# Expert routing of a two-layer block: three bits per round, tile sums by matmul, one-hots of 128 places

## The chip, the cores and the metric

The kernel runs on one core of one Trainium2 chip. A core has a matrix engine (TensorE, PE in the rows, with its weight loads as PEld), VectorE (DVE), ScalarE (ACT), GpSimd (POOL) and SyncE (SP), which here only issues transfers; they share the on-chip SBUF, and TensorE's results stand in PSUM. Engines run their own instruction streams and wait for each other by semaphores. The metric is the device time of the whole kernel in microseconds (us), the median of several executions.

## The reference, cut to what matters

Two layers, each of an attention part and a mixture of eight experts in which every expert picks its tokens. Only the picking is touched by the change:

```python
# layer 0: k = N / E = 256 (softmax over experts, then top_k over tokens); layer 1: k = 2 N / E = 512
route_prob = jax.nn.softmax(xf @ Ws + bs, axis=-1).T      # [E = 8, N = 2048]
route_vals, routes = jax.lax.top_k(route_prob, k)         # per expert: k values and token numbers
xin = xf[routes]
h = jax.nn.gelu(jnp.einsum('ekd,edf->ekf', xin, W1) + b1[:, None, :])
out = jnp.einsum('ekf,efd->ekd', h, W2) + b2[:, None, :]
final = jnp.zeros((N, D)).at[routes.reshape(-1)].add((out * route_vals[..., None]).reshape(-1, D))
```

The order of the tokens within an expert's list doesn't matter, since each result is added back at its token's row. On a tie the lower token number comes first.

## The kernel before

`program` calls one phase after the other: projections, attention, `out_stage` (which leaves the router's logits in `logits`, 128 partitions x 16 tiles of tokens x 8 experts), `route`, `experts`, and the same again for the second layer. Each phase is a block with one hand-written instruction stream per engine, and ends with a barrier of all engines. There is no scheduler: instructions run on each engine in the order in which they are written, and `link(op)` makes VectorE wait for its own operation before the next one starts.

`route` (lines 1069 to 1239) is called with k = 256 (`route0`) and k = 512 (`route1`). Its stream on VectorE:

- softmax over the experts, with the exponential on ScalarE (L1156 to L1162), and the constants `digits` (L1168), 15 multiplications of 128x32.
- Bisection for each expert's k-th largest probability (L1171 to L1183). Probabilities are compared as float32 whose bit pattern is built from the top: two bits in a round, 15 rounds. A round makes four candidates per expert (`cand`), compares all probabilities with them (`above`, 128 x 4 x 16 x 8), lets TensorE sum over partitions and tiles by 16 matmuls with a matrix of ones into `tot` (L1128), keeps the candidates that at least k tokens reach (`passed`) and takes the largest (`kth`).
- Masks of the larger (`ge`) and equal (`eq`) probabilities; `need` is how many of the equal ones are taken.
- `ranks` (L1194 to L1206), called twice: TensorE gives the rank within a tile (`pre`, with a triangular matrix) and each tile's sum (`col`); VectorE adds the sums of earlier tiles by a scan in four doubling steps. The result `pos` is each chosen token's place in its expert's list, -1 for the others.
- The records `rec` (L1219 to L1225), five bfloat16 values for each token and expert: the number within the tile, the tile, the probability in three parts.
- The lists (L1226 to L1239): for each of 8 experts and 16 tiles a one-hot matrix `hot` of 128 tokens x k places (L1230) compares the constant row `slot` (0, 1, 2, ... in float16) with `pos`; TensorE multiplies it, 128 places at a time, with the records (L1142) and sums over the tiles. `hot` has two buffers, and VectorE fills the next expert's while TensorE reads. From `lists` VectorE makes `index` and `weight`, which `experts` reads.

## Time and profile before

| | us |
|---|---|
| median of three timed runs | 4181.79 (4180.73 to 4182.9) |
| the profiled execution | 4189.89 |
| its span, first to last instruction | 4188.3 |
| mean granted TensorE clock | 0.935 of full speed |
| first routing, from its first VectorE operation to its last | 1753.7 to 1828.5 |
| second routing | 3323.6 to 3408.0 |

Times are microseconds from the start of the span. A row of the timeline gives an operation's start, its duration and, in brackets, how long its engine had stood idle before it and who ended that. Operations of one kind in a row are merged (x16), and then the time is that of the whole group. Durations of operations that follow each other without waiting overlap, so the distance between two of them is read from their starts or ends. `128x512 bf16<-128x512 f32` is the shape and type of output and input.

### The profile page before, as it was taken

To read this page: it belongs to the slowest core of one execution; us is meant where nothing else is said; L and a number is where in the kernel's file an instruction comes from. 1 tells how busy PE (TensorE), PEld (TensorE's weight loads), DVE (VectorE), ACT (ScalarE), POOL (GpSimd) and SP (SyncE) were. 2 spreads that over 40 slices of the span, in tenths; PEclk is the share of its full clock that TensorE was granted. 3 is DMA by queue.
4 is the path that set the end of the run, shared out by engine and by line. 5 is a ranking of instruction groups with operands and counts; after the bars stand their busy time and mean duration, and the time that the engine had idled before them with its cause. 6 is when DMAs were issued, how large, how long until landed. Compare 5 with 4: busy or idle time off the path is not lost. (4 is left out here: it accounts for less than half of the span.)

```text
span 4188.3 us, 77504 instructions
## 1 busy us (share of the span) xinstructions
PE 3748.4 (89%) x30860; PEld 2629.4 (63%) x30860; DVE 2555.5 (61%) x3210; ACT 2014.6 (48%) x3511; POOL 1739.5 (42%) x854
## 2 busy tenths in 40 slices
PE   7989799999999996649996699999997649999997
PEld 5768456666666563448995355555553438888886
DVE  4345778888888772566664677777772564433342
ACT  2222266666666662036662366666663024444442
POOL 0000287778777872001110488888884001111110
PEclk9999799999999998669998799999999659999999
DMA  4478624442444223236663522232202233333341
GB/s 161 169 247 284 182 61 106 103 112 63 105 103 112 58 65 117 101 134 205 210 188 111 146 77 77 78 81 78 77 22 80 98 105 120 115 113 113 113 117 29
DMA packets 287917, 485.16 MB, mean 116 GB/s; under 512 B 22289, under 2 KB 117521, under 8 KB 285585
## 3 DMA queue, kind: packets, MB, share of 16 engines
q1 hardware_dynamic: 272016, 443.00, 35.5%
q0 software_dynamic: 14080, 37.76, 3.9%
q8 instruction: 205, 3.36, 0.4%
q14 instruction: 80, 0.65, 0.1%
q10 hardware_dynamic: 1536, 0.40, 0.0%
HBM read 350.67 MB, written 130.02 MB: 115 GB/s over the span
## 5 line engine op out<-in xcount | busy, mean ns | idle before, releaser
L844 DVE TENSOR_REDUCE attn_parts<-attn_mx 128x4 f32<-128x2048 f32 x538 | 1232.6, 2291 | 378.3 <-PE attn_mx L686 378.0
L803 ACT ACTIVATE attn_probs<-attn_low 128x512 f32<-128x512 f32 (+1 forms) x2368 | 1235.1, 595 | 473.0 <-PE attn_low L714 353.2
L665 POOL TENSOR_TENSOR attn_psums<-attn_psums,attn_probs 128x1024 f32<-128x1024 f32 x536 | 1275.2, 2379 | 70.0 <-ACT attn_probs L803 4.8
L714 PE MATMUL attn_low<-attn_queries,attn_keys 97*128 97x256 f32 (+1 forms) x4736 | 917.7, 312 | 13.6 <-ACT attn_probs L803 5.2
L714 PEld LDWEIGHTS attn_low<-attn_queries,attn_keys 97*128 97x128 f32 x4736 | 660.7, 190 | 373.3 <-ACT attn_probs L803 188.8
L731 PE MATMUL attn_low<-attn_probs,attn_values 128*32 128x256 f32 x9472 | 632.2, 385 | 1.4 <-ACT attn_probs L803 1.4
L1462 DVE TENSOR_TENSOR ffn_wL<-ffn_raw,ffn_wH 128x2048 fp32r<-128x2048 f32 x128 | 293.4, 2292 | 224.2 <-ACT ffn_wH L1417 222.9
L1417 ACT ACTIVATE ffn_wH<-ffn_raw 128x2048 fp32r<-128x2048 f32 x128 | 245.2, 1916 | 339.1 <-DMA ffn_raw<-in_L_ffn_W_dram 178.3
L662 POOL TENSOR_TENSOR attn_psums<-attn_probs 128x1024 f32<-128x1024 f32 x88 | 209.6, 2382 | 380.0 <-ACT attn_probs L803 380.0
L731 PEld LDWEIGHTS attn_low<-attn_probs,attn_values 128*32 128x32 f32 x9472 | 248.2, 109 | 183.8 <-issue 3.9
L1374 PE MATMUL ffn_up<-ffn_xH,ffn_wH 128*128 128x256 f32 (+1 forms) x1024 | 350.6, 342 | 2.7 <-DVE ffn_xL L1468 2.7
L686 PE MATMUL attn_mx<-attn_keysn,attn_queriesn 32*128 32x512 f32 (+3 forms) x2388 | 299.6, 494 | 53.1 <-DMA attn_queriesn<-l_queries 28.3
L1374 PE MATMUL ffn_up<-ffn_xH,ffn_wL 128*128 128x256 f32 (+1 forms) x1024 | 346.7, 339 | 0.0
L1374 PE MATMUL ffn_up<-ffn_xL,ffn_wH 128*128 128x256 f32 (+1 forms) x1024 | 346.7, 339 | 0.0
L1389 PE MATMUL ffn_down<-ffn_wH,ffn_hH 128*128 128x512 f32 x768 | 306.7, 399 | 0.0
L1389 PE MATMUL ffn_down<-ffn_wH,ffn_hL 128*128 128x512 f32 x768 | 304.4, 396 | 0.0
L1389 PE MATMUL ffn_down<-ffn_wL,ffn_hH 128*128 128x512 f32 x768 | 304.3, 396 | 0.0
L1343 POOL DMA_INDIRECT out_dram<-ffn_yo,ffn_idx_out x32 | 52.6, 1643 | 594.6 <-DVE ffn_yo L1497 463.5
L738 PE MATMUL attn_low<-attn_probs,keep_onesf 128*32 128x256 f32 (+1 forms) x3776 | 268.5, 375 | 0.0
L1486 DVE TENSOR_TENSOR ffn_hL<-ffn_hf,ffn_hH 128x256 fp32r<-128x256 f32 (+1 forms) x256 | 138.1, 555 | 202.5 <-ACT ffn_hH L1438 199.8
L861 DVE RECIPROCAL attn_inv<-attn_both 128x64 f32<-128x64 f32 x384 | 200.7, 535 | 70.8 <-ACT attn_both L812 70.8
L1438 ACT ACTIVATE ffn_hf<-ffn_up,ffn_b1T 128x256 f32<-128x256 f32 (+1 forms) x256 | 149.2, 583 | 160.7 <-PE ffn_up L1374 156.7
(196 smaller groups left out, 4457.2 us busy)
## 6 DMA issues: line engine op xcount, KB each, us to landing
ffn_raw<-in_L_ffn_W_dram SPq DMA_DIRECT2D x128, 1024.0 KB, 5.6
attn_keys<-l_cross_keys SPq DMA_DIRECT2D x96, 512.0 KB, 6.8
attn_queries<-l_queries SPq DMA_DIRECT2D x48, 512.0 KB, 4.8
l_cross_keys<-projc_high SPq DMA_DIRECT2D x64, 256.0 KB
l_cross_keys<-projc_lowp SPq DMA_DIRECT2D x64, 256.0 KB
l_cross_values<-projc_vout SPq DMA_DIRECT2D x64, 256.0 KB
attn_keysn<-l_cross_keys SPq DMA_DIRECT2D x16, 1024.0 KB, 5.1
attn_values<-l_cross_values SPq DMA_DIRECT2D x32, 512.0 KB, 6.7
```

The costliest lines, as they stand in the source:

```text
L662: pool.tensor_tensor(ps, probs[:, m % RING, 0, :, :], at, ALU.add).then_inc(added, 1)
L665: pool.tensor_tensor(ps, ps, at, ALU.add).then_inc(added, 1)
L686: mm = pe.matmul(room[:, h, at:at + cols], QN[b][rows_h, q0:q0 + P], KN[b][rows_h, part * BLK:part * BLK + cols], start=True, stop=True)
L714: mm = pe.matmul(out[:, n0:], KS[b][0:3 * HD + 1, h, kb * P:(kb + 1) * P], QS[b][0:3 * HD + 1, h, job.qb * QB + n0:(job.qb + 1) * QB], sta ...
L731: mm = pe.matmul(acc[h * HD:(h + 1) * HD, 0, n0:], VS[b][:, kb, h * HD:(h + 1) * HD], probs[:, m % RING, i, h, n0:], start=kb == 0, stop=k ...
L738: mm = pe.matmul(acc[h * HD:(h + 1) * HD, 1, n0:], c["onesf"][:, 0:HD], probs[:, m % RING, i, h, n0:], start=False, stop=False, skip_group ...
L803: act.activation(probs[:, m % RING, i // 2, heads, n0:], sc[:, item % SC, :].rearrange("p (h q) -> p h q", q=QB)[:, :, n0:], ACT.Exp, scal ...
L844: op = dve.tensor_reduce(into, seen, AX.X, ALU.max)
L1374: mm = pe.matmul(up[ft % UP][:, 0:k], w[:, cols], x[:, ch, :], start=n == 0, stop=n == 3 * C - 1)
L1389: mm = pe.matmul(down[st][:, :], h[:, ft, st * P:(st + 1) * P], w[:, cols], start=ft == 0 and n == 0, stop=ft == FT - 1 and n == 2)
L1417: act.activation(wH[:, m % RING, :], raw[:, m % RING, :], ACT.Copy).then_inc(high_made, 1)
L1462: dve.tensor_tensor(wL[:, m % RING, :], raw[:, m % RING, :], wH[:, m % RING, :].bitcast(F32), ALU.subtract).then_inc(low_made, 1)
```

## The change

Only `route` is changed. The bisection takes three bits in a round (`WAYS` = 8 candidates, 10 rounds). `digits` is computed by GpSimd. The masks are written directly as bfloat16. The sums of earlier tiles are added by TensorE: after the triangular matmul, 15 matmuls with ones add each tile's mask to all later tiles in `pre`; `col` and the scan are gone. A token's place is split into `part` (which 128 places of the list) and `place` (0 to 127 in it). The one-hots have 128 places for either k. The records are copied ST = k/128 times, each copy multiplied by whether the token belongs to that part (`recs`), and one matmul for expert and tile gives all parts side by side. `hot` has room for all experts. Experts 6 and 7 are made by ScalarE from `less` = -`place`: |slot - place| by Abs, then max(0, 1 - that) by Relu, each pair with a wait in between. Part of the records' work moves to before the waits for TensorE.

```diff
-    ROUNDS = 15
+    BITS, ROUNDS = 3, 10
+    WAYS = 1 << BITS
+    BY_ACT = (6, 7)
...
+        recs = ph.sb("recs", [P, NTILE, E, ST, NV], BF16)
         tok = ph.sb("tok", [P, 2, NTILE], I32)
-        hot = ph.sb("hot", [P, 2, NTILE, k], BF16)
+        hot = ph.sb("hot", [P, E, NTILE, P], BF16)
+        gap = ph.sb("gap", [P, 2, P])
...
             @block.gpsimd
             def _(pool):
-                pool.iota(digit[:, :, :], pattern=[[1, 4], [0, E]], base=0, channel_multiplier=0)
+                pool.iota(digit[:, :, :], pattern=[[1, WAYS], [0, E]], base=0, channel_multiplier=0).then_inc(numbered, 1)
+                pool.wait_ge(numbered, 1)
+                for n in range(ROUNDS):
+                    pool.tensor_scalar(digits[:, n, :, :], digit[:, :, :], float(WAYS ** (ROUNDS - 1 - n)), None, ALU.mult
+                                       ).then_inc(digits_set, 1)
...
                 act.activation(prob[:, :, :], rest[:, :, :], ACT.Exp).then_inc(expd, 1)
+                act.wait_ge(placed, 1)
+                n = 0
+                for e in BY_ACT:
+                    for t in range(NTILE):
+                        act.activation(gap[:, n % 2, :], c["slot"][:, 0:P], ACT.Abs, bias=less[:, t, e:e + 1]
+                                       ).then_inc(gap_set, 1)
+                        act.wait_ge(gap_set, n + 1)
+                        act.activation(hot[:, e, t, :], gap[:, n % 2, :], ACT.Relu, scale=-1.0, bias=c["onesf"][:, 0:1]
+                                       ).then_inc(hot_act, 1)
+                        n += 1
...
-                for n in range(2):
-                    pe.wait_ge(counted, ROUNDS + 2 + n)
-                    pe.matmul(pre[:, :, :], c["lowerb"][:, :], maskb[:, :, :], start=True, stop=True)
-                    pe.matmul(col[:, :, :], c["onesb"][:, :], maskb[:, :, :], start=True, stop=True
-                              ).then_inc(summed, 1)
+                for n, mask in ((2, eqb), (3, selb)):
+                    pe.wait_ge(counted, ROUNDS + n)
+                    pe.matmul(pre[:, :, :], c["lowerb"][:, :], mask[:, :, :], start=True, stop=False, skip_group_check=True)
+                    for t in range(NTILE - 1):
+                        mm = pe.matmul(pre[:, t + 1:, :], c["onesb"][:, :],
+                                       mask[:, t, :].unsqueeze(1).to_broadcast([P, NTILE - 1 - t, E]),
+                                       start=False, stop=t == NTILE - 2, skip_group_check=True)
+                    mm.then_inc(summed, 1)
+                pe.wait_ge(recs_set, ST)
                 for e in range(E):
-                    pe.wait_ge(hot_ready, e + 1)
-                    for st in range(ST):
-                        for t in range(NTILE):
-                            mm = pe.matmul(lists[:, e, st, :], hot[:, e % 2, t, st * P:(st + 1) * P],
-                                           rec[:, t, e, :], start=t == 0, stop=t == NTILE - 1)
-                    mm.then_inc(hot_used, 1)
+                    if e in BY_ACT:
+                        pe.wait_ge(hot_act, NTILE * (BY_ACT.index(e) + 1))
+                    else:
+                        pe.wait_ge(hot_ready, e + 1)
+                    for t in range(NTILE):
+                        mm = pe.matmul(lists[:, e, :, :], hot[:, e, t, :], recs[:, t, e, :, :],
+                                       start=t == 0, stop=t == NTILE - 1)
+                mm.then_inc(hot_used, 1)
...
+                dve.wait_ge(summed, ROUNDS + 2)
+                link(dve.tensor_tensor(pos[:, :, :], pre[:, :, :], over_tokens(need[:, :]), ALU.is_lt))
+                link(dve.tensor_tensor(pos[:, :, :], pos[:, :, :], eqb[:, :, :], ALU.mult))
+                dve.tensor_tensor(selb[:, :, :], pos[:, :, :], geb[:, :, :], ALU.add).then_inc(counted, 1)
...
+                dve.wait_ge(summed, ROUNDS + 3)
+                link(dve.scalar_tensor_tensor(out=pos[:, :, :], in0=pre[:, :, :], scalar=1.0, in1=selb[:, :, :],
+                                              op0=ALU.add, op1=ALU.mult))
+                link(dve.tensor_scalar(part[:, :, :], pos[:, :, :], float(P + 1), None, ALU.is_ge))
+                for st in range(2, ST):
+                    link(dve.scalar_tensor_tensor(out=part[:, :, :], in0=pos[:, :, :], scalar=float(st * P + 1),
+                                                  in1=part[:, :, :], op0=ALU.is_ge, op1=ALU.add))
+                link(dve.scalar_tensor_tensor(out=rest[:, :, :], in0=part[:, :, :], scalar=float(-P), in1=pos[:, :, :],
+                                              op0=ALU.mult, op1=ALU.add))
+                link(dve.tensor_scalar(less[:, :, :], rest[:, :, :], -1.0, 1.0, ALU.mult, ALU.add))
+                dve.tensor_scalar(place[:, :, :], rest[:, :, :], -1.0, None, ALU.add).then_inc(placed, 1)
+                for st in range(ST):
+                    dve.scalar_tensor_tensor(out=recs[:, :, :, st, :],
+                                             in0=part[:, :, :].unsqueeze(3).to_broadcast([P, NTILE, E, NV]),
+                                             scalar=float(st), in1=rec[:, :, :, :], op0=ALU.is_equal, op1=ALU.mult
+                                             ).then_inc(recs_set, 1)
+                dve.wait_ge(placed, 1)
                 for e in range(E):
-                    if e >= 2:
-                        dve.wait_ge(hot_used, e - 1)
+                    if e in BY_ACT:
+                        continue
                     for t in range(NTILE):
-                        op = dve.tensor_scalar(hot[:, e % 2, t, :], c["slot"][:, 0:k], pos[:, t, e:e + 1], None,
+                        op = dve.tensor_scalar(hot[:, e, t, :], c["slot"][:, 0:P], place[:, t, e:e + 1], None,
                                                ALU.is_equal)
                     op.then_inc(hot_ready, 1)
```

How the engines' streams read at two places of the first routing (names are of tiles, `route_` for this phase, `keep_` for what outlives it). VectorE before, from the end of the second `ranks` to the copy of the lists:

```order
L1206 TENSOR_TENSOR route_pos<-route_scan,route_pre 128x128
L1215 TENSOR_SCALAR route_pos<-route_pos 128x128
L1216 TENSOR_TENSOR route_pos<-route_pos,route_sel 128x128
L1217 TENSOR_SCALAR route_pos<-route_pos 128x128
L1219 CAST route_rec<-route_tok 128x128
L1220 CAST route_rec<-route_tok 128x128
L1221 CAST route_rec<-route_prob 128x128
L1222 TENSOR_TENSOR route_rest<-route_prob,route_rec 128x128
L1223 CAST route_rec<-route_rest 128x128
L1224 TENSOR_TENSOR route_rest<-route_rest,route_rec 128x128
L1225 CAST route_rec<-route_rest 128x128
L1230 TENSOR_SCALAR route_hot<-keep_slot,route_pos 128x256 x128
```

VectorE now, from the last part of the records (which stands behind the mask of the chosen tokens) to the copy of the lists:

```order
L1221 CAST route_rec<-route_rest 128x128
L1225 SCALAR_TENSOR_TENSOR route_pos<-route_pre,route_selb 128x128
L1227 TENSOR_SCALAR route_part<-route_pos 128x128
L1231 SCALAR_TENSOR_TENSOR route_rest<-route_part,route_pos 128x128
L1233 TENSOR_SCALAR route_less<-route_rest 128x128
L1234 TENSOR_SCALAR route_place<-route_rest 128x128
L1236 SCALAR_TENSOR_TENSOR route_recs<-route_part,route_rec 128x128x5 x2
L1245 TENSOR_SCALAR route_hot<-keep_slot,route_place 128x128 x96
L1249 COPY route_got<-route_lists 128x80
```

The records now come ahead of the places, two masked copies of them stand behind, and 96 one-hots of 128 places take the place of 128 of 256 (in the second routing, of 512, with four copies).

ScalarE before, from the exponential into the experts phase:

```order
L1121 ACT_TABLE_LOAD
L1121 ACTIVATE route_prob<-route_rest 128x128
L1111 UNCONDITIONAL_BRANCH
L1402 UNCONDITIONAL_BRANCH
L1417 ACTIVATE ffn_wH<-ffn_raw 128x2048 x3
```

ScalarE now at the same place, up to the first of 32 pairs:

```order
L1124 UNCONDITIONAL_BRANCH
L1127 ACT_TABLE_LOAD
L1127 ACTIVATE route_prob<-route_rest 128x128
L1132 ACTIVATE route_gap<-keep_slot,route_less 128x128
L1135 ACTIVATE route_hot<-route_gap,keep_onesf 128x128
```

The pairs stand behind the exponential in the same phase; the number of table loads is the same as before.

## Rows read from the trace of the kernel before

**Rows 1.** page: span; then busy us (share) xinstructions of each engine
```profile
span 4188.3 us, 77504 instructions
...
PE 3748.4 (89%) x30860; PEld 2629.4 (63%) x30860; DVE 2555.5 (61%) x3210; ACT 2014.6 (48%) x3511; POOL 1739.5 (42%) x854
```

**Rows 2.** stretches: start:end length, busy (xinstructions), clock, DMA share, GB/s
```profile
1753.60:1828.60 75.00, 18.25 (x501) 15.39 (x501) 58.05 (x256) 1.59 (x2) 0.36 (x3) 0.50 0.00 1
3323.60:3408.10 84.50, 25.07 (x757) 22.21 (x757) 66.78 (x256) 1.57 (x2) 0.35 (x3) 0.50 0.01 1
...
3371.00:3406.40 35.40, 14.94 (x512) 14.27 (x512) 33.48 (x128) 0.00 (x0) 0.00 (x0) 0.50 0.01 2
```

**Rows 3.** timeline, one round: start, us, engine line op out<-in xcount [idle]
```profile
1759.72 0.19 DVE L1173 TENSOR_TENSOR route_cand<-route_digits,route_kth 128x32 int32<-128x32 int32 x1
1759.94 0.69 DVE L1175 TENSOR_TENSOR route_above<-route_prob,route_cand 128x512 bf16<-128x512 f32 x1
...
1760.69 0.61 PE L1128 MATMUL route_tot<-route_above,keep_onesb 128*128 128x32 bf16 x16 [1.48 <-DVE route_above L1175]
1761.34 0.19 DVE L1181 SCALAR_TENSOR_TENSOR route_passed<-route_tot,route_cand 128x32 f32<-128x32 f32 x1 [0.71 <-PE route_tot L1128]
```

**Rows 4.** timeline, VectorE, constants and first candidates
```profile
1756.21 1.37 DVE L1168 TENSOR_SCALAR route_digits<-route_digit 128x32 int32<-128x32 int32 x15
1757.53 0.07 DVE L1170 MEMSET route_kth<- 128x8 int32 x1
1757.62 0.19 DVE L1173 TENSOR_TENSOR route_cand<-route_digits,route_kth 128x32 int32<-128x32 int32 x1
```

**Rows 5.** timeline, VectorE, last threshold to one-hots, first routing
```profile
1788.96 0.29 DVE L1186 TENSOR_TENSOR route_ge<-route_prob,route_kth 128x128 f32<-128x128 f32 x1
...
1789.61 0.38 DVE L1189 TENSOR_REDUCE route_count<-route_ge 128x8 bf16<-128x128 f32 x1
...
1798.70 0.34 DVE L1219 CAST route_rec<-route_tok 128x128 bf16<-128x128 int32 x1
1798.84 0.38 DVE L1220 CAST route_rec<-route_tok 128x128 bf16<-128x128 int32 x1
...
1800.86 25.16 DVE L1230 TENSOR_SCALAR route_hot<-keep_slot,route_pos 128x256 bf16<-128x256 f16 x128
```

**Rows 6.** timeline, lists' end of routing one; one-hots, end of two
```profile
1826.07 1.01 PE L1142 MATMUL route_lists<-route_rec,route_hot 128*128 128x5 bf16 x32 [2.12 <-DVE route_hot L1230]
1827.13 0.24 DVE L1234 COPY route_got<-route_lists 128x80 f32<-128x80 f32 x1 [1.11 <-PE route_lists L1142]
...
3370.79 33.69 DVE L1230 TENSOR_SCALAR route_hot<-keep_slot,route_pos 128x512 bf16<-128x512 f16 x128
...
3404.54 1.87 PE L1142 MATMUL route_lists<-route_rec,route_hot 128*128 128x5 bf16 x64 [2.33 <-DVE route_hot L1230]
3406.44 0.33 DVE L1234 COPY route_got<-route_lists 128x160 f32<-128x160 f32 x1 [1.96 <-PE route_lists L1142]
```

**Rows 7.** groups by line and shape, VectorE: xcount | busy us, mean ns
```profile
L1462 DVE TENSOR_TENSOR ffn_wL<-ffn_raw,ffn_wH 128x2048 fp32r<-128x2048 f32 x1 | 2.3, 2293 | 0.4 <-ACT ffn_wH L1417 0.4
```

**Rows 8.** groups by line and shape, GpSimd
```profile
L642 POOL TENSOR_TENSOR attn_y<-attn_both,attn_inv 128x256 f32<-128x256 f32 x96 | 70.5, 734 | 16.8 <-DVE attn_inv L861 16.8
```

**Rows 9.** timeline, ScalarE: routing, first projection, experts
```profile
1753.64 1.28 ACT L1121 ACT_TABLE_LOAD   x1 [12.88 <-PEq L63]
1754.93 0.31 ACT L1121 ACTIVATE route_prob<-route_rest 128x128 f32<-128x128 f32 x1
...
96.86 0.30 ACT L279 ACTIVATE proj_std<-proj_mv,keep_eps 128x4 f32<-128x4 f32 x1 [3.73 <-DVE proj_mv L326]
97.06 0.67 ACT L299 ACTIVATE proj_high<-proj_bank,proj_br 128x512 fp32r<-128x512 f32 x1
...
1992.93 0.47 ACT L1438 ACTIVATE ffn_hf<-ffn_up,ffn_b1T 128x256 f32<-128x256 f32 x1
1993.30 0.47 ACT L1438 ACTIVATE ffn_hH<-ffn_up,ffn_b1T 128x256 fp32r<-128x256 f32 x1
```

More of the change, by code:

```diff
@@ L1075, in route @@
     NV = 5
-    ROUNDS = 15
+    BITS, ROUNDS = 3, 10
+    WAYS = 1 << BITS
+    BY_ACT = (6, 7)
     with Phase(nc, name) as ph:
-        prob, ge, eq, sel, pos = (ph.sb(x, [P, NTILE, E]) for x in ("prob", "ge", "eq", "sel", "pos"))
+        prob, pos, place, part, less = (ph.sb(x, [P, NTILE, E]) for x in ("prob", "pos", "place", "part", "less"))
         rest = ph.sb("rest", [P, NTILE, E])
-        scan = [ph.sb(f"scan{n}", [P, NTILE, E]) for n in range(2)]
-        maskb = ph.sb("maskb", [P, NTILE, E], BF16)
+        geb, eqb, selb = (ph.sb(x, [P, NTILE, E], BF16) for x in ("geb", "eqb", "selb"))
         red = ph.sb("red", [P, NTILE])
         inv = ph.sb("inv", [P, NTILE])
-        count = ph.sb("count", [P, 4, E], BF16)
-        above = ph.sb("above", [P, 4, NTILE, E], BF16)
+        count = ph.sb("count", [P, E], BF16)
+        above = ph.sb("above", [P, WAYS, NTILE, E], BF16)
         need = ph.sb("need", [P, E])
         kth = ph.sb("kth", [P, E], I32)
-        cand = ph.sb("cand", [P, 4, E], I32)
-        passed = ph.sb("passed", [P, 4, E])
-        digit = ph.sb("digit", [P, 4, E], I32)
-        digits = ph.sb("digits", [P, ROUNDS, 4, E], I32)
+        cand = ph.sb("cand", [P, WAYS, E], I32)
+        passed = ph.sb("passed", [P, WAYS, E])
+        digit = ph.sb("digit", [P, WAYS, E], I32)
+        digits = ph.sb("digits", [P, ROUNDS, WAYS, E], I32)
         rec = ph.sb("rec", [P, NTILE, E, NV], BF16)
+        recs = ph.sb("recs", [P, NTILE, E, ST, NV], BF16)
         tok = ph.sb("tok", [P, 2, NTILE], I32)
-        hot = ph.sb("hot", [P, 2, NTILE, k], BF16)
+        hot = ph.sb("hot", [P, E, NTILE, P], BF16)
+        gap = ph.sb("gap", [P, 2, P])
         got = ph.sb("got", [P, E, ST, NV])
@@ L1097, in route @@
         wf = ph.sb("wf", [P, E, ST])
-        tot = ph.ps("tot", (P, 4, E))
+        tot = ph.ps("tot", (P, WAYS, E))
         pre = ph.ps("pre", (P, NTILE, E))
-        col = ph.ps("col", (P, NTILE, E))
         lists = ph.ps("lists", (P, E, ST, NV))
-        chain, counted, summed, expd, hot_ready, hot_used, numbered, max_off = (
-            ph.sem(x) for x in ("chain", "counted", "summed", "expd", "hot_ready", "hot_used", "numbered", "max_off"))
+        (chain, counted, summed, expd, hot_ready, hot_act, hot_used, numbered, digits_set, max_off, placed, recs_set,
+         gap_set) = (
+            ph.sem(x) for x in ("chain", "counted", "summed", "expd", "hot_ready", "hot_act", "hot_used", "numbered",
+                                "digits_set", "max_off", "placed", "recs_set", "gap_set"))
         def over_tokens(tile):
@@ L1162, in _ @@
                 link(dve.tensor_tensor(prob[:, :, :], prob[:, :, :], over_experts(inv[:, :]), ALU.mult))
[L1166 to L1169 removed]
                 link(dve.memset(kth[:, :], 0))
                 for n in range(ROUNDS):
+                    dve.wait_ge(digits_set, n + 1)
                     link(dve.tensor_tensor(cand[:, :, :], digits[:, n, :, :],
[L1174 removed]
+                                           kth[:, :].unsqueeze(1).to_broadcast([P, WAYS, E]), ALU.bitwise_or))
                     dve.tensor_tensor(above[:, :, :, :],
[L1176 to L1177 removed]
+                                      prob[:, :, :].unsqueeze(1).to_broadcast([P, WAYS, NTILE, E]),
+                                      cand[:, :, :].bitcast(F32).unsqueeze(2).to_broadcast([P, WAYS, NTILE, E]),
                                       ALU.is_ge).then_inc(counted, 1)
@@ L1185, in _ @@
                 kthf = over_tokens(kth[:, :].bitcast(F32))
-                link(dve.tensor_tensor(ge[:, :, :], prob[:, :, :], kthf, ALU.is_gt))
-                link(dve.tensor_tensor(eq[:, :, :], prob[:, :, :], kthf, ALU.is_equal))
+                link(dve.tensor_tensor(geb[:, :, :], prob[:, :, :], kthf, ALU.is_gt))
                 with nc.allow_low_precision("small whole numbers"):
-                    dve.tensor_reduce(count[:, 0, :], ge[:, :, :].rearrange("p t e -> p e t"),
+                    dve.tensor_reduce(count[:, :], geb[:, :, :].rearrange("p t e -> p e t"),
@@ L1217, in _ @@
-                link(dve.tensor_scalar(pos[:, :, :], pos[:, :, :], -1.0, None, ALU.add))
+                dve.tensor_tensor(eqb[:, :, :], prob[:, :, :], kthf, ALU.is_equal).then_inc(counted, 1)
+                dve.wait_ge(numbered, 2)
                 dve.tensor_copy(rec[:, :, :, 0], over_experts(tok[:, 0, :]))
```

35 lines of the change are left out of this document (5 added, 30 removed).

## The prediction

> **What bounds the kernel now.** I read the page first: the matrix engine is busy 89% of a span of 4188.3 us [rows 1]. That share is an average, so the next view is the busy time of each engine in the two stretches in which the routing runs [rows 2]. There the picture is another one: in the 75.0 us of the first and the 84.5 us of the second the matrix engine works 18.3 and 25.1 us, the vector engine 58.1 and 66.8, the others almost nothing, and nothing is transferred. No work of another phase lies beside it, since every phase ends with a barrier of all engines. So the routing is 159.5 us of a single chain, mostly on VectorE, and each microsecond taken from that chain comes off the total at full size. The question is only which engine's work makes the chain afterwards.
>
> The timeline of one round [rows 3] shows how it is made: candidates (0.23 us to the next start), the comparison of 128x512 (0.69), 0.05 us of hand-over, 16 matmuls of 32 columns (0.61), a product and a maximum. The next round starts at once; 15 rounds run from 1757.62 [rows 4] to 1788.96 [rows 5], 31.34 us, so 2.09 each. From 1788.96 to the first one-hot at 1800.86 it takes 11.90 us [rows 5]. The second routing runs the same instructions up to there. From the first one-hot to the copy of the finished lists it is 1827.13 - 1800.86 = 26.27 us in the first and 3406.44 - 3370.79 = 35.65 in the second [rows 5, 6].
>
> **Prices that I need.** A VectorE operation with float32 input takes about 0.158 us plus 1.04 ns an element: 0.29 for 128, 0.69 for 512, 2.293 for 2048 [rows 3, 5, 7]. Where the next one waits for it, 0.035 is added; where it does not, only about 0.05 us besides the elements is paid: the two casts of 128x128 end at 1799.04 and 1799.22, 0.18 apart [rows 5]. The matmuls come (0.61 - 0.19)/15 = 0.028 us apart at 32 columns [rows 3] and, with five columns, (1.87 - 1.01)/32 = 0.027 apart [rows 6]; the granted clock is 0.50, the lower level of 1.2 GHz, in both routings [rows 2].
>
> **The constants (off VectorE).** Fifteen multiplications for `digits` lie between 1756.21 and 1757.53 [rows 4] and go to GpSimd as ten of 128x64. There they run beside the softmax. GpSimd's slowest similar row is 0.73 us for 128x256 [rows 8]; ten at even that price end before the last round needs its digits (rounds of 3 us), and the first has 2.5 us from the start of the phase at 1753.6 [rows 9] until it is asked for. Gain: 1.32 x 2 = 2.6 us.
>
> **The rounds.** Ten instead of 15, but with eight candidates instead of four: 80 comparisons of all tokens instead of 60. A round grows by 32 elements in the candidates (+0.03), 512 in the comparison (+0.53), and at 64 columns the matmul distance doubles to 0.056 (15 x 0.028 + 0.03 = +0.45); the product gets +0.03, the strided maximum some +0.05. 2.09 + 1.09 = 3.18, times ten 31.8, against 31.3: a loss of 0.5, for both 0.9 us. The shorter count of rounds is eaten by the wider ones. Bounds: if the matmuls stayed at 0.028 the round were 2.76 (a gain of 3.7 per routing); if loading weights (0.027) no longer hid behind the columns, they would be 0.083 apart and a round 3.6 (+4.1). I take the doubling, because 32 columns already run no slower than the five-column ones.
>
> **From the threshold to the places.** The scan over tiles (nine operations, twice) becomes 15 further matmuls into `pre`: 128 + 960 = 1088 columns at 0.028/32 us, 0.95, with 0.2 of latency 1.15 us. In time from the first comparison: `geb` 0.33, `count` 0.38, `eqb` 0.18, so 0.9; TensorE until 2.1, while VectorE makes the token casts, the first part of the probability and `need` (until 2.0). Then three operations of 0.3 to 3.1, TensorE until 4.3 (the other casts beside it), then the chain to `place`: 0.33 + 0.26 + 0.33 + 0.26 + 0.23 = 1.4. The places stand at 5.7 us; in the second routing two more steps for four parts, 6.4.
>
> **From the places to the lists.** Two engines start side by side.
> VectorE: two (four) masked copies of the records, 640 elements, 0.72 each, then 96 one-hots. A one-hot with 256 places costs 25.16/128 = 0.197, with 512 places 33.69/128 = 0.263 [rows 5, 6]; 256 places are 0.066, so 128 cost 0.164. Together 1.4 + 15.7 = 17.2 us, second routing 18.6. (Were it 0.20, it would still be under ScalarE's time.)
> ScalarE: 32 times a pair Abs, Relu, where Relu waits for its own Abs. An ACTIVATE from SBUF without a pointer takes 0.31 at 128 columns; one with a pointer for the bias 0.30 at four columns, so 0.40 at 128 [rows 9]. How soon the next may start behind one that it does not wait for: 0.20 behind the four columns, so 0.30; or 0.37 behind 256 columns from PSUM, so 0.26 [rows 9]. I take 0.28. Thirty-two times 0.40 + 0.035, 31 times 0.28, and 0.40: 23.0 us. ScalarE is later than VectorE by 5.8 and 4.4 us, so it sets the end. Behind it come 16 matmuls (waits 0.1, 15 x 0.027 + 0.17): 0.7. Matmuls with 10 or 20 columns stay under the distance of 0.027.
>
> First routing: 5.7 + 23.7 = 29.4 against 11.90 + 26.27 = 38.2, a gain of 8.8. Second: 6.4 + 23.7 = 30.1 against 47.6, a gain of 17.5.
>
> **Sum.** -2.6 + 0.9 - 8.8 - 17.5 = -28.0 us. The profiled execution took 4189.9 us (span 4188.3), the median of the three timed ones 4181.8; on the profiled one this makes 4161.9, on the median 4153.8, and I forecast the latter. What follows each routing (barrier, weight loads, gathers) waits for it as before and only moves forward; the matrix engine starts it at the same low clock.
>
> The split of the one-hots is the weak place. By the rows VectorE alone would need 1.4 + 128 x 0.164 = 22.4 us for all 128 (23.9 in the second routing), ScalarE needs 23.0 for a quarter of them. With all of them on VectorE the sum would be -28.0 - 0.6 + 0.9 = -27.7: the hand-over brings about nothing. The Trainium skill (ScalarE: Activation LUTs, Rules for kernel authors) speaks against this part of the change: relu and an addition belong on VectorE, up to three times as fast per element in bf16. By that rule the last part would be as quick without ScalarE; by the change's idea it would be a quarter shorter than VectorE's 22.4.
>
> **Rivals.**
> 1. *ScalarE is quick and VectorE sets the end.* If the pointer's cost hides, a pair is 0.31 + 0.035 + 0.21 = 0.55, all of them 17.7 us, level with VectorE's 17.2 in the first routing and under its 18.6 in the second. The gain grows by 5.3 + 4.4, to -37.7: 4144. For it: in a row of ScalarE's operations latencies are partly covered. Against: the wait between Abs and Relu lays the latency open in every pair.
> 2. *Nothing overlaps on ScalarE.* A pair is 2 x (0.40 + 0.035) = 0.87, 27.8 us: +4.8 twice, -18.4: 4163.
> 3. *The wide rounds are dearer:* matmuls 0.083 apart, +4.1 twice, -19.8: 4162. Against it the equal distances at 5 and 32 columns.
> 4. *Slower than before.* If the change between two functions, or the wait of ScalarE for its own write, costs a pair more than 23.0/32 = 0.72 plus (28.0 + 8.4)/64 = 0.57, so 1.29 us, the kernel is slower by more than 0.2%. A table load is the row with such a price, 1.28 [rows 9]; one at each switch would be 128 x 1.28 = 164 us: 4318. Against it: in the order of the changed program stands one load ahead of the whole sequence and none between Abs and Relu.
> That the change does not do what it says I exclude: the order shows ten rounds and 96 + 32 one-hots.
>
> **How the numbers follow.** Forecast 0.60; rivals 1 to 3: 0.13, 0.13, 0.08; rival 4: 0.03; something unseen that uses up the gain: 0.03. About 0.2% (8.4 us) is what a measurement can tell from no change, so faster 0.94, same 0.03, slower 0.03. The range must hold 0.8: from rival 1's 4143 to 4166, above rivals 2 and 3, which leaves out rival 4, the unseen, and a meeting of rivals 2 and 3 (4171).
>
> **What would show it.** A round in the changed profile: start to start 3.18 us, the 16 matmuls 1.05. GpSimd's ten operations over before the third round. From the first comparison to `place` about 5.7 and 6.4 us. On ScalarE 32 pairs 0.72 apart; VectorE done 5 us before it and then waiting for the lists; the last 16 matmuls right behind ScalarE. The two routing stretches would be about 65.3 and 66.1 us instead of 75.0 and 84.5. I am wrong if VectorE, not ScalarE, ends last, if a pair is far from 0.72, or if the wide rounds are cheaper than 3 us.

## The result, and the profile after

| | before | changed |
|---|---|---|
| median of six timed runs, us | 4183.05 (4180.73 to 4185.65) | 4154.33 (4153.65 to 4154.79) |
| ratio, 95% interval | | 0.9931 [0.9921, 0.9941] |
| span of the profiled execution | 4188.3 | 4152.6 |
| routing 1, first operation to last | 74.8 | 65.8 |
| routing 2 | 84.4 | 66.5 |

The change saves 28.7 us by the medians, 0.7%. The two routings by themselves give 26.95 us of it (159.25 to 132.30 in the two profiles). The spans differ by 35.7 us: the 8.7 more lie outside the routings, mostly ahead of the first one, which starts at 1745.9 us instead of 1753.7 though nothing is changed there. Over all profiled executions of this study the part outside the routings, which is the same program in all of them, varied between 4014 and 4029 us. The two longest (before with 4029.1, b3_scan_vector with 4028.2) have the lowest mean granted clock, 0.935 and 0.936, the two shortest (c2 and c3, 4014.3 and 4014.9) the highest, 0.942; the others lie between without a clear order, and which is the cause of which no run shows. So sizes below are read from the routing stretches, whose unchanged parts repeat within 0.2 us (once 0.4), and the medians only confirm them.

The page of the changed kernel, span and busy times, beside [rows 1]:

```profile
span 4152.6 us, 76276 instructions
...
PE 3735.0 (90%) x30244; PEld 2619.5 (63%) x30244; DVE 2522.6 (61%) x3040; ACT 2059.7 (50%) x3639; POOL 1749.9 (42%) x874
```

Busy times of the two routing stretches, beside [rows 2] (stretch, length, PE, PEld, DVE, ACT, POOL, granted clock, DMA share, GB/s):

```profile
1745.90:1811.80 65.90, 17.27 (x321) 14.87 (x321) 44.25 (x169) 23.86 (x66) 4.84 (x13) 0.50 0.00 1
3305.40:3372.00 66.60, 17.36 (x321) 14.89 (x321) 46.77 (x173) 23.88 (x66) 4.85 (x13) 0.50 0.00 1
```

VectorE has 44.3 and 46.8 us of work left of 58.1 and 66.8, ScalarE has 23.9 instead of 1.6, and the granted clock is 0.50 as before.

One round of the changed kernel, timeline, beside [rows 3]:

```profile
1754.94 0.22 DVE L1188 TENSOR_TENSOR route_cand<-route_digits,route_kth 128x64 int32<-128x64 int32 x1
1755.20 1.22 DVE L1190 TENSOR_TENSOR route_above<-route_prob,route_cand 128x1024 bf16<-128x1024 f32 x1
...
1756.48 1.03 PE L1144 MATMUL route_tot<-route_above,keep_onesb 128*128 128x64 bf16 x16 [2.13 <-DVE route_above L1190]
1757.55 0.23 DVE L1196 SCALAR_TENSOR_TENSOR route_passed<-route_tot,route_cand 128x64 f32<-128x64 f32 x1 [1.13 <-PE route_tot L1144]
1757.81 0.27 DVE L1198 TENSOR_REDUCE route_kth<-route_passed 128x8 f32<-128x64 f32 x1
```

From candidates at 1754.94 to the next ones at 1758.11 a round takes 3.17 us instead of 2.09: the comparison 1.22 instead of 0.69, the matmuls 1.03 instead of 0.61. Ten take 31.9 and 31.7 us, 15 had taken 31.3.

GpSimd's ten products, and VectorE at the start of the rounds, beside [rows 4]:

```profile
1746.19 5.01 POOL L1119 TENSOR_SCALAR route_digits<-route_digit 128x64 int32<-128x64 int32 x10
...
1748.48 0.07 DVE L1185 MEMSET route_kth<- 128x8 int32 x1
1748.58 0.22 DVE L1188 TENSOR_TENSOR route_cand<-route_digits,route_kth 128x64 int32<-128x64 int32 x1
```

Each product takes 0.50 us on GpSimd, and they end at 1751.2, before the second round asks for its own at 1751.8. The 1.3 us between the softmax and the rounds are gone.

From the last threshold to the copy of the lists, VectorE in the first routing, beside [rows 5, 6]:

```profile
1780.47 0.29 DVE L1201 TENSOR_TENSOR route_geb<-route_prob,route_kth 128x128 bf16<-128x128 f32 x1
...
1786.06 0.23 DVE L1234 TENSOR_SCALAR route_place<-route_rest 128x128 f32<-128x128 f32 x1
1786.20 1.60 DVE L1236 SCALAR_TENSOR_TENSOR route_recs<-route_part,route_rec 128x640 bf16<-128x640 f32 x2
1787.69 15.69 DVE L1245 TENSOR_SCALAR route_hot<-keep_slot,route_place 128x128 bf16<-128x128 f16 x96
1810.33 0.24 DVE L1249 COPY route_got<-route_lists 128x80 f32<-128x80 f32 x1 [6.95 <-PE route_lists L1164]
```

The same stretch on TensorE (the tile sums, twice, and the last matmuls of the lists):

```profile
1781.51 1.02 PE L1153 MATMUL route_pre<-route_eqb,keep_onesb 128*128 128x120 bf16 x15
...
1783.72 1.02 PE L1153 MATMUL route_pre<-route_selb,keep_onesb 128*128 128x120 bf16 x15
...
1809.71 0.59 PE L1164 MATMUL route_lists<-route_recs,route_hot 128*128 128x10 bf16 x16 [5.25 <-ACT route_hot L1135]
```

ScalarE's first pair, the Abs of the second, and its last operation:

```profile
1786.32 0.40 ACT L1132 ACTIVATE route_gap<-keep_slot,route_less 128x128 f32<-128x128 f16 x1 [38.84 <-DVE route_place L1234]
1786.76 0.40 ACT L1135 ACTIVATE route_hot<-route_gap,keep_onesf 128x128 bf16<-128x128 f32 x1
1787.06 0.39 ACT L1132 ACTIVATE route_gap<-keep_slot,route_less 128x128 f32<-128x128 f16 x1
...
1809.25 0.40 ACT L1135 ACTIVATE route_hot<-route_gap,keep_onesf 128x128 bf16<-128x128 f32 x1
```

The places stand 5.8 us after the first comparison; before, the one-hots began after 11.9. From the places to the lists it takes 24.0 us. VectorE is done at 1803.4 and then sits idle for 6.95 us: ScalarE's last Relu ends at 1809.65, TensorE's last 16 matmuls start 0.06 later, and only behind them can VectorE copy. ScalarE's pairs come 0.725 us apart (31 distances from the Relu at 1786.76 to the one at 1809.25): Abs 0.39, 0.03 until Relu, and 0.31 from Relu's start to the next Abs.

The second routing, VectorE, beside the second half of [rows 6]:

```profile
3339.85 0.29 DVE L1201 TENSOR_TENSOR route_geb<-route_prob,route_kth 128x128 bf16<-128x128 f32 x1
...
3346.09 0.23 DVE L1234 TENSOR_SCALAR route_place<-route_rest 128x128 f32<-128x128 f32 x1
3346.23 3.38 DVE L1236 SCALAR_TENSOR_TENSOR route_recs<-route_part,route_rec 128x640 bf16<-128x640 f32 x4
3349.49 15.68 DVE L1245 TENSOR_SCALAR route_hot<-keep_slot,route_place 128x128 bf16<-128x128 f16 x96
3370.38 0.33 DVE L1249 COPY route_got<-route_lists 128x160 f32<-128x160 f32 x1 [5.21 <-PE route_lists L1164]
```

Here it is 6.5 and 24.1 us. Before it was 11.9 and 35.65, since each one-hot had 512 places; now both routings take the same, because the 32 pairs don't depend on k.

### The profile page after: what moved, and what is told of

Its sections match the earlier page's. It is cut to its first block and busy times, and to the rows that moved or that the text cites. A ratio compares the mean times of both kernels' runs of the same rounds, so it can differ in the third digit from the quotient of the medians.

```text
span 4152.6 us, 76276 instructions
## 1 busy us (share of the span) xinstructions
PE 3735.0 (90%) x30244; PEld 2619.5 (63%) x30244; DVE 2522.6 (61%) x3040; ACT 2059.7 (50%) x3639; POOL 1749.9 (42%) x874
## 5 line engine op out<-in xcount | busy, mean ns | idle before, releaser
L686 PE MATMUL attn_mx<-attn_keysn,attn_queriesn 32*128 32x512 f32 (+3 forms) x2388 | 299.1, 494 | 51.0 <-DMA attn_queriesn<-l_queries 26.2
```

The lines of the kernel that those rows point to most:

```text
L686: mm = pe.matmul(room[:, h, at:at + cols], QN[b][rows_h, q0:q0 + P], KN[b][rows_h, part * BLK:part * BLK + cols], start=True, stop=True)
```

## The experiments

The theory: the routing is one open chain; its pieces add up; what the fewer rounds save, their greater width takes back; ScalarE's chain of pairs sets the end of the lists, by the latency that each pair's wait lays open. All eleven kernels start from the changed one. This table gives for each the parts of the two routings in us, read from its timelines (softmax: from the first operation to the first candidates; places: from the first comparison with the last threshold to the end of `place`, or to the first one-hot where there is none; lists: from there to the copy of the lists).

| kernel | softmax | rounds | places | lists | both routings | median |
|---|---|---|---|---|---|---|
| before | 4.0, 4.0 | 31.3, 31.3 | 11.9, 11.9 | 26.3, 35.7 | 159.3 | 4183.1 |
| changed | 2.7, 2.7 | 31.9, 31.7 | 5.8, 6.5 | 24.0, 24.1 | 132.3 | 4154.3 |
| a1_one_expert | 2.7, 2.7 | 31.9, 31.9 | 5.8, 6.5 | 20.8, 22.6 | 127.7 | 4148.9 |
| a2_no_scalar | 2.7, 2.7 | 31.9, 31.7 | 5.8, 6.5 | 23.0, 24.7 | 131.9 | 4152.1 |
| a3_abs_ahead | 2.7, 2.7 | 31.9, 31.8 | 5.8, 6.5 | 19.5, 20.4 | 124.1 | 4144.0 |
| b1_two_bits | 2.7, 2.7 | 31.5, 31.3 | 5.8, 6.5 | 24.0, 24.1 | 131.5 | 4153.4 |
| b2_digits_vector | 3.7, 3.7 | 31.7, 31.7 | 5.8, 6.5 | 24.0, 24.1 | 134.2 | 4153.1 |
| b3_scan_vector | 2.7, 2.7 | 31.9, 31.8 | 10.4, 11.1 | 24.0, 24.1 | 141.5 | 4161.1 |
| b4_wide_hots | 2.7, 2.7 | 31.9, 31.7 | 5.0, 5.0 | 26.3, 35.7 | 143.9 | 4159.3 |
| c1_seven | 2.7, 2.7 | 29.2, 29.1 | 5.8, 6.5 | 24.1, 24.1 | 127.0 | 4148.6 |
| c2_seven_halves | 2.7, 2.7 | 26.2, 26.3 | 5.8, 6.5 | 24.1, 24.1 | 121.2 | 4142.5 |
| c3_best | 2.7, 2.7 | 26.2, 26.3 | 5.8, 6.5 | 19.5, 20.4 | 113.0 | 4130.6 |
| c4_best_two_bits | 2.7, 2.7 | 26.8, 26.8 | 5.8, 6.8 | 19.5, 20.4 | 114.5 | 4134.8 |

The medians are of four runs, before and changed of six; the kernel before had 4179.7 beside the a kernels and b1, 4179.4 beside b2 to c1, and 4182.6 beside the last three. The changed kernel itself was not run again beside them, and the four runs of one kernel spread by up to 18 us (a1: 4136.2 to 4153.9). So a median against 4154.3 can be wrong by several microseconds (b4's expected total was 4165.8, its median is 4159.3, while its routings came as expected), and the expectations are judged by the routings.

**a1_one_expert: less work for ScalarE.**

```diff
-    BY_ACT = (6, 7)
+    BY_ACT = (7,)
```

> ScalarE makes the one-hots of one expert (7) instead of two; VectorE makes 112 instead of 96. Theory (ScalarE's chain of pairs, 0.725 us each, sets the end of the lists): ScalarE needs 11.6 us, VectorE 1.4 + 112 x 0.163 = 19.7 in the first routing and 21.5 in the second, and the stretch from the places to the copy of the lists falls from 24.0 to 20.8 and 22.6 us; total 4.7 us below the changed kernel, about 4149.6. Rival (VectorE or the matmuls set the end, ScalarE's late finish costs nothing): 16 more one-hots on VectorE make it 2.6 us longer per routing, 4159.5.

The end of the lists in the first routing, VectorE:

```profile
1791.33 18.28 DVE L1245 TENSOR_SCALAR route_hot<-keep_slot,route_place 128x128 bf16<-128x128 f16 x112
1810.72 0.24 DVE L1249 COPY route_got<-route_lists 128x80 f32<-128x80 f32 x1 [1.11 <-PE route_lists L1164]
```

VectorE does 16 one-hots more (18.28 us instead of 15.69), and the lists are done 3.2 and 1.5 us sooner. VectorE's idle time falls from 6.95 to 1.11 us, what 32 matmuls take. The rival falls: the late end was ScalarE's.

**a2_no_scalar: nothing for ScalarE.**

```diff
-    BY_ACT = (6, 7)
+    BY_ACT = ()
```

> All 128 one-hots on VectorE. Theory: 1.4 + 128 x 0.163 + 0.7 = 23.0 us instead of 24.0 in the first routing, 3.2 + 20.9 + 0.7 = 24.7 instead of 24.1 in the second; total within 0.5 us of the changed kernel, so ScalarE's quarter brings nothing. Rival (ScalarE's quarter is worth a quarter of VectorE's work): 5.2 us more per routing, 4164.7.

The first routing, VectorE:

```profile
1786.92 20.88 DVE L1245 TENSOR_SCALAR route_hot<-keep_slot,route_place 128x128 bf16<-128x128 f16 x128
1808.48 0.24 DVE L1249 COPY route_got<-route_lists 128x80 f32<-128x80 f32 x1 [0.68 <-PE route_lists L1164]
```

All 128 one-hots take 20.88 us on VectorE, 0.163 each. The lists need 23.0 us (24.0 with ScalarE's quarter) and 24.7 (24.1): together 0.4 us less than the changed kernel, as expected to the tenth. ScalarE's share as the change gives it brings nothing.

**a3_abs_ahead: the same pairs, the latency covered.**

```diff
-        gap = ph.sb("gap", [P, 2, P])
+        gap = ph.sb("gap", [P, 4, P])
...
+                tiles = [(e, t) for e in BY_ACT for t in range(NTILE)]
+                for n in range(len(tiles) + 1):
+                    if n < len(tiles):
+                        e, t = tiles[n]
+                        act.activation(gap[:, n % 4, :], c["slot"][:, 0:P], ACT.Abs, bias=less[:, t, e:e + 1]
+                                       ).then_inc(gap_set, 1)
+                    if n > 0:
+                        e, t = tiles[n - 1]
+                        act.wait_ge(gap_set, n)
+                        act.activation(hot[:, e, t, :], gap[:, (n - 1) % 4, :], ACT.Relu, scale=-1.0,
+                                       bias=c["onesf"][:, 0:1]).then_inc(hot_act, 1)
```

> ScalarE issues the next pair's Abs ahead of the Relu that waits for its own Abs, with four buffers between them instead of two; the same 64 operations. Theory (the pair's 0.725 us are the open latency of Abs, 0.39 us, which the wait lays bare, plus one distance of 0.31): the pair falls to two distances, 0.56 to 0.62 us, ScalarE's part from 23.3 to 18 to 20, about level with VectorE; places to lists 19.3 to 20.7 and 20.3 to 21.5 us, total 6 to 8.5 us lower. Rival (0.725 is what two such operations cost on ScalarE in any order): no change, 4154.

ScalarE in the middle of its pairs, and the copy of the lists (places at 1786.7 in this execution):

```profile
1787.59 0.39 ACT L1133 ACTIVATE route_gap<-keep_slot,route_less 128x128 f32<-128x128 f16 x1
1787.88 0.38 ACT L1138 ACTIVATE route_hot<-route_gap,keep_onesf 128x128 bf16<-128x128 f32 x1
1788.17 0.39 ACT L1133 ACTIVATE route_gap<-keep_slot,route_less 128x128 f32<-128x128 f16 x1
1788.46 0.39 ACT L1138 ACTIVATE route_hot<-route_gap,keep_onesf 128x128 bf16<-128x128 f32 x1
...
1806.17 0.24 DVE L1251 COPY route_got<-route_lists 128x80 f32<-128x80 f32 x1 [2.42 <-PE route_lists L1166]
```

The operations last as long as before, 0.39, but start 0.29 apart: a pair is 0.583 us instead of 0.725. The lists come 4.5 and 3.7 us sooner. This separates the two theories: the price of a pair is not fixed by its two operations. It is one distance and one open latency, and the latter can be hidden by order alone. In the first routing TensorE's last matmuls still wait for ScalarE, in the second for VectorE's last one-hot (3361.31 against 3361.29 for ScalarE): the two engines are level, as expected.

**b1_two_bits: the rounds as before.**

```diff
-    BITS, ROUNDS = 3, 10
+    BITS, ROUNDS = 2, 15
```

> The changed kernel with two bits in a round and 15 rounds, as before the change (GpSimd still makes the constants, 15 of 128x32). Theory (the wide rounds bring nothing): 15 x 2.09 = 31.3 us instead of 31.8, total 1 us below the changed kernel. Rival (the three bits carry part of the gain, by a third of the rounds): 5 rounds of 2.09 more, 10.4 us per routing, 4175.

Rounds 31.5 and 31.3 us instead of 31.9 and 31.7. Three bits in a round, by themselves, are a loss of 0.4 us per routing, and the rival (a gain of 10.4) falls.

**b2_digits_vector: the constants back on VectorE.** The loop over `digits[:, n, :, :]` moves from GpSimd's stream to VectorE's, ahead of the rounds.

> The changed kernel with the ten products for the digits back on VectorE, ahead of the rounds. Theory: the part before the first candidates grows from 2.67 us by 10 x 0.11 to 0.12 to about 3.8; total +2.3 us. Rival (GpSimd's work beside the softmax slows VectorE as much as it saves): no change.

The products and what follows them in the first routing, VectorE:

```profile
1748.81 1.11 DVE L1184 TENSOR_SCALAR route_digits<-route_digit 128x64 int32<-128x64 int32 x10
1749.87 0.07 DVE L1186 MEMSET route_kth<- 128x8 int32 x1
```

Ten products cost 1.06 us (1748.81 to 1749.87), so 0.11 each on VectorE against 0.50 on GpSimd, where they are free because nothing waits for them. The routings are 1.9 us longer (the part before the first candidates 1.0 each, less 0.15 for a pause in the changed kernel's rounds, see the end). The rival falls: beside GpSimd's work one operation of the softmax is 0.04 us longer. The median of four runs (4153.1) is too coarse to show it.

**b3_scan_vector: the tile sums by the scan.**

```diff
-                    for t in range(NTILE - 1):
-                        mm = pe.matmul(pre[:, t + 1:, :], c["onesb"][:, :],
-                                       mask[:, t, :].unsqueeze(1).to_broadcast([P, NTILE - 1 - t, E]),
-                                       start=False, stop=t == NTILE - 2, skip_group_check=True)
-                    mm.then_inc(summed, 1)
+                    pe.matmul(col[:, :, :], c["onesb"][:, :], mask[:, :, :], start=True, stop=True
+                              ).then_inc(summed, 1)
...
+                def ranks():
+                    link(dve.tensor_copy(scan[0][:, :, :], col[:, :, :]))
+                    at, by = 0, 1
+                    while by < NTILE:
+                        old, new = scan[at], scan[1 - at]
+                        dve.tensor_copy(new[:, 0:by, :], old[:, 0:by, :])
+                        link(dve.tensor_tensor(new[:, by:, :], old[:, by:, :], old[:, 0:NTILE - by, :], ALU.add))
+                        at, by = 1 - at, 2 * by
...
```

> The changed kernel with the tile sums made as before: one matmul for the tile sums and the scan on VectorE, twice; the rest as changed. Theory: the nine operations of the scan cost 2.5 us each time, TensorE is done 0.7 us earlier, which was hidden the first time and 0.3 the second; from the threshold to the places 10.4 us instead of 5.8 (11.1 instead of 6.5 in the second routing), total +9.2 us, 4163. Rival (16 dependent accumulating matmuls of up to 128 columns cost nearly as much as the scan): +2 us at most.

First comparison and `place` in the first routing:

```profile
1790.64 0.29 DVE L1211 TENSOR_TENSOR route_geb<-route_prob,route_kth 128x128 bf16<-128x128 f32 x1
...
1800.82 0.23 DVE L1246 TENSOR_SCALAR route_place<-route_rest 128x128 f32<-128x128 f32 x1
```

10.41 us instead of 5.82 (11.07 instead of 6.47): the tile sums on TensorE are worth 4.6 us in each routing.

**b4_wide_hots: one-hots of k places.** Everything behind `pos` as in the kernel before: one buffer pair `hot` of 128 x k, plain records, no masks, no `part`, nothing on ScalarE.

> The changed kernel with the one-hots as before: 128 of k places on VectorE, two buffers, unmasked records, one matmul for each 128 places; rounds, digits and tile sums as changed. Theory: from the threshold to the first one-hot 4.9 us, from there to the copy of the lists 26.3 and 35.7 us as before the change; routing 1.4 and 10.1 us longer than changed, total +11.5 us, 4165.8: nearly all of the gain of the narrow one-hots lies in the second routing. Rival (masked copies and ScalarE's pairs eat the gain in both): +3 us at most in the second.

The second routing:

```profile
3343.16 33.70 DVE L1219 TENSOR_SCALAR route_hot<-keep_slot,route_pos 128x512 bf16<-128x512 f16 x128
...
3378.82 0.33 DVE L1223 COPY route_got<-route_lists 128x160 f32<-128x160 f32 x1 [1.96 <-PE route_lists L1151]
```

33.70 us of one-hots as before the change, lists after 35.7. The routings are 1.4 and 10.15 us longer than in the changed kernel. The narrow one-hots, as the change makes them, pay almost only where k is 512. This run undoes width, masked copies and ScalarE's share together. From the threshold to the lists the first routing takes 31.3 us here, 29.9 in the changed kernel, 28.8 with the narrow one-hots on VectorE alone (a2) and 25.3 in a3_abs_ahead. So with k = 256 they pay too, once ScalarE's latency is covered.

**c1_seven: without the candidate that always passes.** Candidate 0 of a round is the present threshold.

```diff
-        above = ph.sb("above", [P, WAYS, NTILE, E], BF16)
+        above = ph.sb("above", [P, WAYS - 1, NTILE, E], BF16)
...
+                    dve.tensor_copy(passed[:, 0, :], kth[:, :].bitcast(F32))
...
-                    link(dve.scalar_tensor_tensor(out=passed[:, :, :], in0=tot[:, :, :], scalar=float(k),
+                    link(dve.scalar_tensor_tensor(out=passed[:, 1:, :], in0=tot[:, :, :], scalar=float(k),
```

> The changed kernel without the candidate 0 of each round, which is the present threshold and always passes: seven candidates are compared and summed, the present threshold is copied into the maximum's input behind the comparison. By the price of a candidate (0.133 us on VectorE, 16 x 0.0067 on TensorE, and small things) a round falls from 3.17 to 2.91 us, ten of them from 31.8 to 29.2; total -5.2 us, 4149. Rival (the added copy of 128x8 lies on the path): 2.98, -3.8 us.

29.15 us for ten rounds, 2.7 and 2.6 less than in the changed kernel (2.6 without the pause in its first routing); the copy is not on the path: the price of a candidate, taken from the rows of the two widths, holds for a third width.

**c2_seven_halves: TensorE beside the comparison.**

```diff
+                    for h in range(2):
+                        tiles = slice(h * NTILE // 2, (h + 1) * NTILE // 2)
+                        dve.tensor_tensor(above[:, :, tiles, :],
+                                          prob[:, tiles, :].unsqueeze(1).to_broadcast([P, WAYS - 1, NTILE // 2, E]),
...
+                        if t % (NTILE // 2) == 0:
+                            pe.wait_ge(counted, 2 * n + 1 + t // (NTILE // 2))
```

> c1_seven with the comparison made in two halves of eight tiles, so that TensorE sums the first half while VectorE compares the second. Theory: only 8 of the 16 matmuls stay open (0.54 us instead of 0.93) and the extra instruction costs 0.05: a round 2.58 us instead of 2.91, ten 25.8 instead of 29.15, total -6.7 us against c1_seven. Rival (the hand-over is paid twice and the matmuls slow the comparison): at best -2 us.

26.2 and 26.3 us for the rounds, 2.9 less per routing than with one comparison, where 3.4 were expected. A round is 2.61 instead of the expected 2.58, since the second instruction costs the comparison 0.07 us (1.16 instead of 1.09) and not 0.05, and one round of the second routing has a pause of 0.16. The rival (at best -2 in total) falls: it is -5.8.

**c3_best: both, and Abs ahead.**

> c2_seven_halves with ScalarE's Abs issued ahead as in a3_abs_ahead. Theory: the two gains add, since the stretches follow each other: rounds 25.8 us, places to lists 19.5 and 20.4; the routings 55.2 and 56.8 us, together 112 instead of 132.3 (changed) and 159.3 (before); about 4134 us if the changed kernel is at 4154, a ratio of about 0.9885 to before. Rival (they do not add): over 4141.

A round of it, timeline:

```profile
1754.96 0.22 DVE L1203 SCALAR_TENSOR_TENSOR route_passed<-route_tot,route_cand 128x56 f32<-128x56 f32 x1 [0.57 <-PE route_tot L1147]
...
1755.51 0.22 DVE L1191 TENSOR_TENSOR route_cand<-route_digits,route_kth 128x56 int32<-128x56 int32 x1
1755.76 1.16 DVE L1195 TENSOR_TENSOR route_above<-route_prob,route_cand 128x448 bf16<-128x448 f32 x2
...
1756.44 1.09 PE L1147 MATMUL route_tot<-route_above,keep_onesb 128*128 128x56 bf16 x16 [1.52 <-DVE route_above L1195]
1756.84 0.16 DVE L1200 COPY route_passed<-route_kth 128x8 f32<-128x8 f32 x1
1757.57 0.22 DVE L1203 SCALAR_TENSOR_TENSOR route_passed<-route_tot,route_cand 128x56 f32<-128x56 f32 x1 [0.57 <-PE route_tot L1147]
```

The round is 2.61 us (1754.96 to 1757.57). TensorE starts at 1756.44, while VectorE is still comparing, and VectorE waits 0.57 us for it instead of 1.13 in the changed kernel and 0.94 in c1_seven. The routings take 55.5 and 57.4 us, together 112.95. The gains add: 11.15 us of c2 and 8.2 of a3 are 19.35, and the rival falls. The ratio to before is 0.9881 [0.9865, 0.9898], 4130.6 against 4182.6 us: this is the quickest version of the study, 19.4 us of routing below the changed kernel.

**c4_best_two_bits: the same with two bits.**

> c3_best with two bits in a round (three candidates, 15 rounds). Theory: the matmuls are at their least distance of 0.027 already at 24 columns, so leaving out a candidate saves only VectorE's 0.14; a round 1.79 us, 15 of them 26.9, so 1.1 us a routing longer than three bits. Rival (the price is the number of candidates alone, 45 against 70): 15 x 1.70 = 25.5, level with three bits or quicker.

A round of it, timeline:

```profile
1754.82 0.18 DVE L1203 SCALAR_TENSOR_TENSOR route_passed<-route_tot,route_cand 128x24 f32<-128x24 f32 x1 [0.41 <-PE route_tot L1147]
...
1755.50 0.63 DVE L1195 TENSOR_TENSOR route_above<-route_prob,route_cand 128x192 bf16<-128x192 f32 x2
...
1755.91 0.66 PE L1147 MATMUL route_tot<-route_above,keep_onesb 128*128 128x24 bf16 x16 [1.13 <-DVE route_above L1195]
...
1756.61 0.18 DVE L1203 SCALAR_TENSOR_TENSOR route_passed<-route_tot,route_cand 128x24 f32<-128x24 f32 x1 [0.41 <-PE route_tot L1147]
```

A round is 1.79 us, as expected, and 15 are 26.8, 0.7 and 0.5 more than c3_best's ten; 1.1 were expected, because c3's own rounds had been put at 25.8. The rival (25.5) falls. The second lot of eight matmuls waits for the second comparison, which ends at 1756.13, and is done 0.44 us later, at 1756.57. With 0.05 of hand-over, seven distances of 0.027 and 0.18 for the last one 0.42 were to be expected, with distances a quarter shorter 0.37. So matmuls of 24 columns come no closer to each other than those of 32 did, and leaving out a candidate saves nothing on TensorE here: two bits lose slightly.

## Why the prediction was right, point by point

The forecast was 4153.8 us, the median is 4154.33. That they agree within 0.5 us is partly luck. The forecast took 28.0 us off a median of three runs, 4181.79; the kernel before has 4183.05 over six, and the measured gain is uncertain by about 4 us. What was really forecast well is the routings: 26.95 us of gain for 28.0. By its steps:

- *The routing is one chain and nothing else moves.* Right. The gain of both routings, 26.95 us, appears in the medians (28.7, interval 24.7 to 33.0). That nothing else moves can't be read closer than this interval: what profiles show outside of the routings varies by up to 15 us.
- *The constants: -2.6.* 2.67 instead of 3.95 us twice, -2.6. b2 adds that ten products of the new width would have cost VectorE 1.06, not 1.32.
- *The rounds: +0.9.* +0.55 and +0.41, 3.17 us a round for a forecast of 3.18. b1 shows the loss by itself (+0.4 twice). The doubling of the matmuls' distance was the disputed piece: 1.03 us for 16 at 64 columns against a computed 1.06. Rival 3 (columns and weight loads in series, a round of 3.6) falls.
- *Threshold to places: 5.7 and 6.4.* 5.82 and 6.47, together 0.2 more. The 15 accumulating matmuls took 1.02 us beside the first one.
- *The masked records and 96 one-hots: 17.2 us.* 17.1 (1786.29 to 1803.38); 0.163 a one-hot, forecast as 0.164 from 256 and 512 places. In the second routing 18.85 for 18.6: four masked copies took 3.26 us (3346.23 to 3349.49), 0.82 each and not 0.72, which cost nothing under ScalarE's time.
- *ScalarE: 23.0 and 0.7.* 23.4 from the places to the last Relu (a1 and a3 show that it is this chain that ends last) and 0.7 behind it. The largest miss: the distance between a Relu and the next Abs was taken as 0.28 between two rows, 0.26 and 0.30; it is 0.31, while Abs and hand-over are 0.42 instead of 0.435. So a pair is 0.725 instead of 0.715, and ScalarE's part 0.3 to 0.4 us longer. In the two routings that is 0.7 of the 1.05 us by which they gained less than the 28.0 forecast; 0.2 lie ahead of the places, the rest are hundredths.
- *Rival 1 (ScalarE is quick).* It fell as stated. a3 brings about what it forecast, by another order: with Abs ahead the pair is 0.583 (0.55 in the rival), the engines are level, and the routings gain 35.2 us (37.7 in the rival).
- *Rival 2 (nothing overlaps)* fell: 0.31 of the 0.40 of a Relu are all that the next Abs waits for.
- *Rival 4 (a price of 1.29 us a pair)* fell: between the end of an Abs and its Relu lie 0.03 us, and in a3 Abs and Relu in turn start 0.29 apart. So neither the wait nor the change of functions has a price near that, apart from the open latency.
- *The split of the one-hots brings about nothing.* Forecast -27.7 without ScalarE against -28.0 with it; a2 measured 131.9 against 132.3, so by 0.4 us it is rather a loss, where a gain of 0.3 was forecast. The rule of the Trainium skill (ScalarE: Activation LUTs, Rules for kernel authors) is to keep relu and additions on VectorE. This case's traces agree for this split: a one-hot costs VectorE 0.163 us and ScalarE 0.725; the page's factor of up to three per element in bf16 no run here tests. a3 shows where the rule stops: as a helper beside a busy VectorE, with the latency hidden, ScalarE saves 3.5 and 4.3 us of the lists against VectorE alone.

Undone one by one, the parts are worth 1.9 (constants), -0.8 (rounds), 9.2 (tile sums) and 11.6 us (one-hots, records and ScalarE together), 21.9 in sum. Of the other 5 us, 0.7 are the constants again (fifteen products before, ten in b2), 4.6 lie between threshold and places, and the rounds take back 0.1 (a loss of 0.96, of which b1 undoes 0.82). As to the places: b4, with the wide one-hots, takes 5.0 us there instead of 11.9, and the tile sums explain 4.6 of the 6.9 in each routing. The rest, 2.3 a routing, must be the edits that no run undid alone. By the rows it is mostly the records' casts, which stood on the path for 2.2 us (1798.70 to 1800.86 in [rows 5]) and now lie beside TensorE's sums; how much the masks written as bfloat16 and the fused operations add is not shown.

## What to carry to other kernels

In a stage that is one chain between barriers, a sum of rows (elements times price, plus one latency for each operation that is waited for) can forecast a rewrite closely; here it missed the gain by 4%. Write the price of a round as a fixed part and a part per candidate before trading rounds for width: here 1.01 us and 0.27 for each candidate (from 2.09 with four and 3.17 with eight), so 15 narrow and 10 wide rounds cost nearly the same. When work is shared out to a second engine, multiply its own latency by the number of its waits first: a pair whose second operation waits for the first costs ScalarE 0.725 us, and 0.583 when another pair's operation lies between the two. A candidate whose answer is known, and a sum that can start on half the input, were worth more than the extra bit.

## What was not expected of the hardware

- A product of 128x64 int32 values takes 0.50 us on GpSimd and 0.11 on VectorE in a row of ten; for the forecast it was bounded from above only, by 0.73. Any price that lets the first product end within 2.4 us, and each further one within a round, would have done.
- While GpSimd ran beside the softmax, the subtraction of 128x128 on VectorE took 0.33 us instead of 0.29 (b2, without that work: 0.29). It is a few hundredths in all.
- In the first routing the fourth of the ten rounds of the changed kernel has a pause between the maximum and the next candidates: the maximum starts at 1760.98 and lasts 0.27, the candidates start at 1761.44, so 0.19 us lie between, where all other rounds have 0.03. It explains 31.9 against 31.7 us. It recurs: a1, a2, a3, b1, b3 and b4 have it in the same round, and a1 has one in the fifth round of its second routing too. c2 and c3 have it in the third round of the second routing instead, b2 (the one without GpSimd's products), c1 and c4 in none. In c4 VectorE waits 0.4 us longer for TensorE between threshold and places of its second routing. The cause stays open.
